# Pair loop of a state-space mixer: TensorE's order of work in a pair, and when VectorE reads the pair outputs

## The reference

```
Bh = rope(repeat(rms(B)) + B_bias, phi);  Ch = rope(repeat(rms(C)) + C_bias, phi)
phi = cumsum(dt)[..., None] * rope_freqs; u = xh * dt[..., None]
h = a_t * h + u_t * b_t                   # state, 8 x 64 a head
y = einsum('bhpn,bhn->bhp', h, c_t)
y = scale * ys + D_param * xh             # then gate, norm, projection
```

## Time and profile before

| | |
|---|---|
| runs shown, median (lowest, highest) | 1589.98 us (1587.69, 1592.98) |
| profiled execution | 1585.28 us |
| its span, first to last instruction | 1583.5 us |
| mean granted clock of PE | 0.914 of 2.4 GHz |
| busy over the span: PE, DVE, ACT, POOL | 85%, 70%, 57%, 28% |
| pair loops | from about 431 to 744 us and from about 1208 to 1520 us |

### The profile page before, as it was taken

One profiled execution on the slowest core, in us unless ns is written; L12 is line 12 of the kernel. 1 busy time (PEld: TensorE's weight loads), 2 busy tenths in 40 slices (PEclk: granted clock), 3 DMA queues, 4 the chain that ended last, 5 costly groups with the idle time before them and its releaser, 6 DMA issues.

```text
span 1583.5 us, 39619 instructions
## 1 busy us (share of the span) xinstructions
PE 1345.4 (85%) x15816; PEld 800.9 (51%) x15816; DVE 1115.0 (70%) x1799; ACT 907.9 (57%) x1523; POOL 448.7 (28%) x421
## 2 busy tenths in 40 slices
PE   5688888898689999998846889888977999999994
PEld 3533332345366666665535333323444676666663
DVE  4677862445389999996565678632354999999937
ACT  3524457533478888884417244563344888888741
POOL 4799920231222222222124000002321222222201
PEclk9689999898689999999967799999987999999997
DMA  5000001300522222221010000000015222222200
GB/s 165 1 2 2 2 7 31 106 1 14 120 55 55 53 60 60 53 54 28 14 54 1 29 2 2 2 1 27 11 36 101 65 58 53 53 53 58 50 2 27
DMA packets 37614, 62.04 MB, mean 39 GB/s; under 512 B 15088, under 2 KB 25072, under 8 KB 36992
## 3 DMA queue, kind: packets, MB, share of 16 engines
q1 hardware_dynamic: 37216, 58.44, 15.4%
q10 hardware_dynamic: 288, 2.10, 0.3%
HBM read 19.75 MB, written 7.01 MB: 17 GB/s over the span
## 4 chain that ended last, share of the span: by engine, by line
PE 56%; issue 14%; DVE 13%; ACT 12%; DVEq 2%; POOL 2%; POOLq 1%; ACTq 1%
DVE region L1186 5%; PE PS L1530 4%; PE PS L1777 4%; PE PS L1640 4%; PE PS L1592 4%; PE PS L1652 4%; PE PS L1793 3%; PE PS L1762 3%; ACT L1018 3%; PE PS L1542 3%; PE PS L1810 2%; PE PS L1881 2%; PE PS L1572 2%; PE PS L1734 2%; PE PS L1685 2%
## 5 line engine op out<-in xcount | busy, mean ns | idle before, releaser
L795 POOL TENSOR_TENSOR region<-region 128x1024 f32<-128x1024 f32 x64 | 153.1, 2393 | 490.1 <-DVE region L1327 490.1
L890 ACT ACTIVATE region<-PS 128x512 f32<-128x512 f32 x288 | 165.1, 599 | 128.1 <-PE PS L1592 86.6
L1186 DVE TENSOR_REDUCE region<-PS 128x1 f32<-128x512 f32 (+3 forms) x304 | 180.8, 654 | 73.6 <-PE PS L1545 40.4
L1777 PEld LDWEIGHTS PS<-region 64*64 64x64 f32 x4096 | 136.5, 135 | 39.5 <-issue 39.5
L1777 PE MATMUL PS<-region 64*64 64x64 f32 x4096 | 154.1, 223 | 0.0
L1542 PE MATMUL PS<-region 96*128 96x512 bf16 (+3 forms) x384 | 117.1, 357 | 26.8 <-DVE region L1186 19.3
L1592 PE MATMUL PS<-region 99*128 99x512 bf16 x288 | 112.1, 410 | 20.1 <-ACT region L890 19.2
L1332 DVE TENSOR_TENSOR region<-region 128x1024 f32<-128x1024 f32 x64 | 117.4, 1834 | 0.1
L723 POOL TENSOR_TENSOR coef<-var,power 128x4 f32<-128x4 f32 (+2 forms) x16 | 16.2, 1011 | 333.3 <-DVEq L1103 333.3
L1010 ACT COPY region<-PS 128x512 f32<-128x512 f32 x128 | 74.8, 585 | 60.5 <-PE PS L1762 60.2
L996 ACT ACT_TABLE_LOAD x60 | 77.0, 1283 | 50.8 <-PE PS L1737 35.4
(11 more groups left out here) (260 smaller groups left out, 2999.6 us busy)
## 6 DMA issues: line engine op xcount, KB each, us to landing
region<-region SPq DMA_DIRECT2D x256, 128.0 KB, 2.3
region<-parts_scratch SPq DMA_DIRECT2D x8, 448.0 KB, 7.6
X<-in_L_attn_x_dram SPq DMA_DIRECT2D x2, 1024.0 KB, 5.5
region<-in_L_ffn_factors_dram SPq DMA_DIRECT2D x2, 1024.0 KB, 6.9
out_dram<-X SPq DMA_DIRECT2D x4, 512.0 KB, 2.9
parts_scratch<-region SPq DMA_DIRECT2D x2, 768.0 KB, 3.3
w_in_s<-in_L_attn_W_in_dram SPq DMA_DIRECT2D x1, 1216.0 KB, 7.7
region<-in_L_ffn_W_fc_dram SPq DMA_DIRECT2D x1, 1024.0 KB, 5.8
```

The costliest lines, as they stand in the source:

```text
L795: nc.gpsimd.tensor_tensor(PB1[:, r], PB1[:, r], PB2, ALU.add).then_inc(s_bb, 1)
L890: nc.scalar.activation(PB[:, u % (2 * G0), :], PS[:, 2 + u % 2, :], ACT.Exp).then_inc(s_p, 1)
L1186: nc.vector.reduce_max(MB[:, h:h + nh, k0 // 4], src, AX).then_inc(s_smu, 1)
L1777: last = mm(PS[q, 2 + half, (i % 4) * P + 64 * c:(i % 4) * P + 64 * c + 64], PB1[q, r, t], PC1[q, r, t], start=True, stop=True, tile_posit ...
```

## The change

On PE a slot's order becomes: outputs of the pair before, first turn, decay arguments, second turn, both Gram halves in one block, turned outputs of the pair before, chunk sums, phases. On DVE `pair_outputs` is split in two: `add_carried`, which reads the turned outputs from PSUM into YT, goes ahead of the C sum, and `add_direct`, which adds YT to the direct term, stays behind it. The products' wait for the outputs of two pairs before (`s_yt`) moves from ahead of the B products to ahead of the C products. The same instructions run, in the same number and shapes.

```diff
@@ products
-
-                    dve.wait_ge(s_yt, at(b, n, 2))
                     g = lambda j: rows[:, j, bass.ds(n, 1)]
                     nc.vector.scalar_tensor_tensor(PB1[:, k % 2], XV[:, 0], g(0), T1[:, k % 2], ALU.add, ALU.mult)
                     nc.vector.scalar_tensor_tensor(PB2, XV[:, 1], g(1), T2[:, k % 2], ALU.add, ALU.mult)
+
+                    dve.wait_ge(s_yt, at(b, n, 2))
@@
-                def pair_outputs(n):
+                def add_carried(n):
 
                     dve.wait_ge(s_yi, at(b, n + 1))
                     e = ELT[:, :, bass.ds(n * 2, 4)].unsqueeze(3).to_broadcast([P, NT, 4, HD])
                     y = PS[:, 7, :].rearrange("p (y t e d) -> p y t e d", y=2, t=NT, d=HD)
+                    nc.vector.tensor_tensor(YT, y[:, 0], e, ALU.mult)
+                    dve.drain()
+                    nc.vector.tensor_tensor(YT, YT, y[:, 1], ALU.add)
+
+                def add_direct(n):
+
                     own = XS[:, :, bass.ds(n * 16, 32)].rearrange("p t (e d) -> p t e d", d=HD)
                     d = dpar[:, bass.ds(n * 2, 4)].unsqueeze(1).unsqueeze(3).to_broadcast([P, NT, 4, HD])
-                    nc.vector.tensor_tensor(YT, y[:, 0], e, ALU.mult)
                     nc.vector.tensor_tensor(own, own, d, ALU.mult)
-                    dve.drain()
-                    nc.vector.tensor_tensor(YT, YT, y[:, 1], ALU.add)
                     dve.drain()
                     nc.vector.tensor_tensor(own, own, YT, ALU.add).then_inc(s_yd, 2)
@@ slots of DVE
                             mixing(n - 1, k + 3)
+                        if k % 2 == 1 and not (first and k == 1):
+                            add_carried(n - 3)
                         rotated_c(n, k)
                         if k % 2 == 1 and not (first and k == 1):
-                            pair_outputs(n - 3)
+                            add_direct(n - 3)
@@ slots of PE
                         decay_args(it, k, not (last_ and k >= 2))
+                        turn(n, k, 1)
                         gram(n, k, 0)
-                        turn(n, k, 1)
                         gram(n, k, 1)
+                        if not (first and k == 0):
+                            turn_outputs(n - 1, k + 3)
                         chunk_sums(n, k)
...
                             phases(it + 1, k - 1)
-                        if not (first and k == 0):
-                            turn_outputs(n - 1, k + 3)
```

More of the change, by code:

```diff
@@ L1376, in _ @@
                 mixing(PAIRS - 1, 3)
-                pair_outputs(PAIRS - 2)
+                add_carried(PAIRS - 2)
+                add_direct(PAIRS - 2)
                 def gate(i):
```

## The result

The changed kernel took 1567.73 us (median of four runs, 1562.83 to 1569.48), beside 1588.84 us (four runs, 1584.67 to 1592.98) of the kernel before. The ratio is 0.9881, 95% interval 0.9848 to 0.9913: about 21 us faster, where 4.4 were forecast. The profiled execution ran 1568.87 us, with a span of 1567.1. In the changed kernel the lines of PE are six higher than before; on DVE the products are L1322, L1323, L1326 and L1327, the C sum is still L1332, `add_carried` L1353 and L1355, `add_direct` L1361 and L1363.

The account below looks back on a forecast made before the run. DVE was taken to pace both pair loops, PE with ACT afterwards. Per batch 1.4 us in the loop, 0.8 start, 0.4 last pairs and −0.5 end gave 2.1 to 2.3, 4.4 for two: 1585.6 us, range 1576 to 1593.

Parts of the forecast that it names:

- PE's slot: PE in the pair loop: handovers keep their sum, only joining the Gram halves saves; 8.82 us, bound 8.94.
- the join's 0.12: Joining the Gram halves on PE replaces one 0.15 us handover by 0.03, saving 0.12 us a slot.
- Waits for sines: PE waits for ACT's sines: 1.04 us at k (pair number modulo 4) 0 and 1, 0.33 at 2, 0 at 3.
- Who sets the pace: In the pair loop after the change, PE and ACT together, at 37.69 us a pass, above DVE's 36.58.
- DVE's pass: DVE's four slots of one loop iteration fall from 37.92 to 36.58 us, each odd slot 0.67 shorter.
- Chunk sums: PE's chunk sums come 0.67 us later, so their 0.27 wait for ACT goes and DVE's scan waits longer.
- Start, last pairs, end: Gains per batch outside the loop: 0.8 us at the start, 0.4 in the last four pairs, −0.5 at the end.
- Rival 1: ACT hides its sines and DVE stays the pacer: pass near 36.58 us, 1572.5 us in all; chance 0.08.
- Rival 2: Joining PE's Gram halves saves nothing: slot 8.94 us, pass 38.05, about 1591 us in all; chance 0.20.
- Rival 3: PE's clock falls in its new waits: over 0.3% slower from six falls, 1606 us at twelve; chance 0.08.

Follow-up runs that it names:

- narrowed turned outputs: Changed kernel with each product of the turned outputs cut in two of half the width (128x32 tiles): 1567.6 us, one run.
- DVE relieved: Changed kernel with POOL's B sum cut to 8 of its 1024 columns: 1562.8 us, one run, pass 36.63 us.
- ACT ahead: Changed kernel with ACT starting a one-column sine before its wait for the phases and laying out inputs in halves: 1563.6 us, pass 36.30 us.

## Why the prediction was wrong

**The step that failed** is PE's slot, in the sentence "The other handovers change partners; a handover goes by what is leaving the array (0.3 behind 512 columns, 0.15 behind narrow products), so I keep their sum". It priced the new order at the join's 0.12 a slot: 8.82, with 8.94 as the other bound. Start to start, where nothing is waited for, the slot went from 8.94 to 8.45. The handovers of both traces, medians where nothing is waited for:

| handover | tiles | before, us | after, us |
|---|---|---|---|
| outputs, first turn | 128*32, 128*128 | 0.203 | 0.203 |
| first turn, decay arguments | 128*128, 112*128 | 0.109 | 0.109 |
| decay arguments, Gram | 128*128, 64*64 | 0.309 | |
| decay arguments, second turn | 128*128, 128*128 | | 0.219 |
| Gram, second turn | 64*64, 128*128 | 0.149 | |
| turn, Gram | 128*128, 64*64 | 0.202 | 0.202 |
| Gram, chunk sums or turned outputs | 64*64, 128*64 | 0.148 | 0.149 |
| turned outputs, chunk sums | 128*64, 128*64 | | 0.005 |
| chunk sums, phases | 128*64, 96*128 | 0.135 | 0.135 |
| phases, turned outputs or outputs | 96*128, 128*64 or 128*32 | 0.309 | 0.309 |
| turned outputs, outputs | 128*64, 128*32 | 0.151 | |
| sum | | 1.715 | 1.331 |

The sum falls by 0.384; the joined Gram block is 0.045 shorter (1.911 from its first to its last start, two halves had 0.978 each), and the second turn, behind decay arguments instead of Gram products, 0.057: 0.486 a slot, 1.94 a pass. In the prediction's terms, 0.37 a slot was missing. What leaves the array matters, but so does whether the next kind needs another tile: behind products of 512 columns the next start comes after 0.22 with the same tile and after 0.31 with another, and behind the narrow ones after 0.005 or after about 0.15. With the whole array (128*128, 112*128 and 96*128) counted as one tile, the old order changes it eight times a slot, the new one five times. The Trainium skill has the rule (TensorEngine Tiling (Array Packing), "Key Properties"): changing the tiling mode, and not just the tile, drains TensorE. The narrowed turned outputs agree, with 0.005 against 0.149. The prediction didn't weigh the tile, though the earlier trace rows show it.

With 8.45 the prediction's own working gives 4 × 8.45 + 2 × 1.04, and at k = 2 a wait of 10.32 − (9.99 − 0.37) = 0.70: 36.58 a pass, measured 36.65. That it comes so close is in part luck. The waits for sines were 2.51 a pass and not 2.78, and two waits that the prediction put at 0 make up for it: 0.14 for ACT's second copy ahead of the chunk sums at k = 3, and 0.15 for DVE's scan ahead of the outputs at the loop's turn. The forecast's other terms, one by one:

- **Waits for sines.** Forecast 1.04, 1.04, 0.33 and 0 at k = 0 to 3; measured 0.88, 1.04, 0.59 and 0 (medians over both batches). Right in place, and nearly in size; the 0.59 is larger because PE's shorter slots come sooner to ACT's late sines, which the 0.70 shows.
- **Who sets the pace.** PE and ACT together, as forecast: with DVE relieved the pass stayed, with ACT ahead it fell to DVE's.
- **DVE's pass.** Forecast 36.58, measured 36.3 where ACT runs ahead of its sines; the moved wait, 0.26 to 0.29 a pass in the kernel before, is as large as the difference. It is hidden in the changed kernel, as the kernel without that move shows. Odd C sums 1.22, YT not stretched: right.
- **Chunk sums.** DVE stands for the chunk sums (0.3, once a pass): right. The wait for ACT's copy is gone at k = 0 and 2, as forecast, but at k = 3 0.14 of it is left.
- **Start, last pairs, end.** Forecast +0.8, +0.4 and −0.5 a batch; measured +1.7 and +1.1, +0.9 twice, −0.4 twice. The end was right. The first two may carry the same mis-sized slot, but PE's order alone gave only 0.7 and 0.5 at the start, and they were not taken apart.

**The rivals.** Rival 1 gave 1572.5 and a pass of 36.58. The number nearly came true, the mechanism didn't: the sines are not hidden, and DVE doesn't set the pace. The rule of the Trainium skill beside it, to shorten the engine of highest occupancy (Perfetto Trace Analysis, "Identifying the Most-Contended Engine"), held for the kernel before, since PE's order alone gave nothing; in the changed kernel DVE is still busier than PE's weight loads (35.36 against 25.70 in the pass), and relieving it left the pass where it was (36.63), so there it misleads. Rival 2 was the same term, mis-sized to the other side: passes of 37.5 came only with the halves apart. Rival 3 didn't occur.

What the change does, then: the earlier read of the outputs takes the odd C sums out from beside POOL, for which the turned outputs must come early; the order that makes them early would cost PE 1.0 us of sines a slot at k = 0 and 1, and pays for it by three changes of tile less a slot. In numbers, a pass of PE stands 2.5 us for sines, 0.5 before, and its four slots are 1.94 shorter. The price of a change between other tiles than those measured here was not tried.

## What to carry to other kernels

Where PE works off many short blocks of products, count how often the tile changes from block to block and price each change from the rows; where the data allow it, put blocks of the same tile next to each other. When two engines are near a tie, undo the parts of a change one by one and together: here each part alone gave −0.3 to +0.6 us a pass, and two together −1.3. And before an instruction is moved ahead, look for who still reads its buffer: a wait that was covered by work in between shows in full.

## What the hardware showed beyond that

- A one-column sine ahead of a wait moves a table load of 1.28 us out of the way for 0.20 us of ACT: sines start 0.42 us after the last phase product's start instead of 1.77 (600.26 − 598.49 in the changed kernel).
- Moving a single wait on DVE, without any change of what is waited for in the end, shortened the standing time between a C sum and the next first product from 0.33 to 0.23 us (3.0 and 2.1 us in nine times, from 510 to 672 us), and the kernel by 0.5% (interval 0.2 to 0.75) where DVE set the pace. Why the wait's place matters was not tried.
